# Cross-attention on one core: three GpSimd helpers of two instructions each become six of one, called in another order

## The reference, cut to what matters

```python
Q = (q @ Wq + bq).reshape(b, s, H, DH).transpose(0, 2, 1, 3)   # q = x
K = (k @ Wk + bk) ...; V = (v @ Wv + bv) ...                   # k = v = ctx
scores = jnp.einsum('bhqd,bhkd->bhqk', Q, K) / jnp.sqrt(jnp.float32(DH)) * mask
attn = jax.nn.softmax(scores, axis=-1)
ctx = jnp.einsum('bhqk,bhkd->bhqd', attn, V).transpose(0, 2, 1, 3).reshape(b, s, H * DH)
x = q + (ctx @ Wo + bo)
out = (x - mean(x)) * rsqrt(var(x) + LN_EPS) * gamma + beta
```

## Time and profile before

| | |
|---|---|
| median of 3 runs | 2428.19 us (2426.65 to 2430.57) |
| the profiled execution | 2422.3 us |
| its span, first to last instruction | 2420.5 us |
| TensorE busy | 2191.4 us, 91% |
| VectorE busy | 2016.7 us, 83% |
| ScalarE busy | 1792.0 us, 74% |
| GpSimd busy | 1100.5 us, 45% |

### The profile page before, as it was taken

How to read it: one execution, slowest core, us unless ns; L and a number is a source line. 1 busy time by engine, 2 the same in 40 slices (tenths; PEclk the granted TensorE clock), 3 DMA queues, 4 the chain that set the end, 5 groups by cost and what they waited for, 6 DMA issues and landing times.

```text
span 2420.5 us, 46357 instructions
## 1 busy us (share of the span) xinstructions
PE 2191.4 (91%) x12348; PEld 902.9 (37%) x12348; DVE 2016.7 (83%) x4283; ACT 1792.0 (74%) x3809; POOL 1100.5 (45%) x1576
## 2 busy tenths in 40 slices
PE   3789999999999999999999999999999999999995
PEld 1233433334333333433334333333433334333442
DVE  6798988889888888888889888888888889889892
ACT  3688786877868677786877868677786877868781
POOL 2134363544626355363544636355363544536434
PEclk9899999999999999999999999999999999999997
DMA  5388877687777868677687777868677687777774
GB/s 204 74 147 153 167 139 175 117 183 145 155 148 140 183 123 184 137 139 174 123 180 144 155 151 142 176 123 181 140 140 174 124 180 147 149 151 138 161 133 106
DMA packets 1117594, 363.28 MB, mean 150 GB/s; under 512 B 1073504, under 2 KB 1073504, under 8 KB 1117408
## 3 DMA queue, kind: packets, MB, share of 16 engines
q1 hardware_dynamic: 1114288, 361.58, 72.3%
q10 hardware_dynamic: 3120, 0.01, 0.1%
HBM read 76.30 MB, written 16.78 MB: 38 GB/s over the span
## 4 chain that ended last, share of the span: by engine, by line
PE 43%; ACT 17%; issue 17%; POOL 13%; DVE 7%; DMA 2%; ACTq 1%; POOLq 1%; DVEq 0%; SPq 0%
PE fill_ps L389 10%; PE fill_ps L390 9%; PE fill_ps L391 9%; PE score_ps L442 8%; ACT probs L614 7%; PE ctx_ps L463 6%; ACT p L628 5%; DVE p L939 3%; POOL neg_max L1234 2%; POOL raw L1214 2%; POOL acc L1276 2%; DVE score_ps L925 2%; ACT v L593 1%; DMA pT<-p 1%; POOL acc L1278 1%
## 5 line engine op out<-in xcount | busy, mean ns | idle before, releaser
L614 ACT ACTIVATE probs<-score_ps,neg_max 128x512 f32<-128x512 f32 x1024 | 694.5, 685 | 340.0 <-POOL neg_max L1234 295.5
L925 DVE CUSTOM_DVE_ANT_0 score_ps<-score_ps,mask_sb,small 128x512 f32<-128x512 f32 x1024 | 730.1, 752 | 72.3 <-PE score_ps L442 41.9
L939 DVE SCALAR_TENSOR_TENSOR p<-probs,inv_sum,p 128x512 f16<-128x512 f32 x896 | 758.3, 879 | 26.4 <-ACT p L628 26.4
L628 ACT ACTIVATE p<-probs,inv_sum 128x512 f16<-128x512 f32 x1024 | 681.3, 723 | 36.0 <-DVE inv_sum L933 33.6
L442 PE MATMUL score_ps<-k,q 64*128 64x512 f16 x3072 | 455.9, 387 | 142.7 <-ACT probs L614 135.8
L1234 POOL TENSOR_SCALAR neg_max<-row_max 128x2 f32<-128x2 f32 x512 | 179.0, 350 | 662.3 <-DVE row_max L925 659.4
L463 PE MATMUL ctx_ps<-pT,v 128*64 128x512 f16 x3072 | 360.8, 385 | 13.9 <-DMA pT<-p 12.4
L442 PEld LDWEIGHTS score_ps<-k,q 64*128 64x128 f16 x3072 | 142.5, 94 | 435.0 <-ACT probs L614 278.7
L1240 POOL TENSOR_SCALAR down_sum<-row_sum 128x4 f32<-128x4 f32 x256 | 74.5, 291 | 423.7 <-ACT probs L614 415.8
L463 PEld LDWEIGHTS ctx_ps<-pT,v 128*64 128x64 f16 x3072 | 166.3, 111 | 201.3 <-issue 72.5
L614 ACT ACTIVATION_READ_ACCUMULATOR probs<-score_ps,neg_max 128x1 f32 x1024 | 205.1, 200 | 0.0
(11 more groups left out here) (91 smaller groups left out, 3006.0 us busy)
## 6 DMA issues: line engine op xcount, KB each, us to landing
raw<-in_xt SPq DMA_DIRECT2D x64, 256.0 KB, 4.1
raw<-in_ct SPq DMA_DIRECT2D x64, 256.0 KB, 3.4
mask_sb<-in_mask_Bx1xSxS_fk SPq DMA_DIRECT2D x64, 256.0 KB, 3.1
acc<-in_x SPq DMA_DIRECT2D x64, 256.0 KB, 3.2
out<-acc SPq DMA_DIRECT2D x64, 256.0 KB, 2.5
pT<-p SPq DMA_TRANSPOSE x512, 4.5
wq_staged<-in_L_xattn_Wq SPq DMA_DIRECT2D x4, 512.0 KB, 6.9
wk_staged<-in_L_xattn_Wk SPq DMA_DIRECT2D x4, 512.0 KB, 10.8
```

The costliest lines, as they stand in the source:

```text
L614: nc.scalar.activation(probs[:, i % E_TILES, :], score_ps[:, i % 4, :], ACT.Exp, bias=neg_max[:, p % 2, i:i + 1], accum_out=row_sum[:, p % ...
L628: nc.scalar.activation(p16[:, q, a, 0, :], probs[:, i % E_TILES, :], ACT.Copy, scale=inv_sum[:, p % 2, i:i + 1]).then_inc(p_rounded, 1)
L925: nc.vector.tensor_tensor_reduce(out=score_ps[:, i % 4, :], in0=score_ps[:, i % 4, :], in1=mask_sb[:, q, :], scale=score_scale, scalar=-3. ...
L939: nc.vector.scalar_tensor_tensor(out=p16[:, q, a, 1, :], in0=probs[:, i % E_TILES, :], scalar=inv_sum[:, p % 2, i:i + 1], in1=p16[:, q, a, ...
```

## The change

`split_input` (L1214, L1217), `split_probs` (L1247, L1252) and `scale_and_shift` (L1276, L1278) are each cut in two. The new helpers are `scale_input` and `split_input`, `normalize_probs` and `split_probs`, `scale_out` and `shift_out`. No instruction is added or taken away, and each keeps its own waits. What differs is the place: GpSimd's `body` now calls the halves apart, and some negations of row maxima and scalings of sums stand between them. The other engines' programs are the same.

```diff
-            def split_input(n, t, tiles):
+            def scale_input(n, t, tiles):
...
+            def split_input(n, t, tiles):
+                for i in tiles:
                     wait_alone(pool, xc_scaled[t], n * DT + i + 1)
...
                 if here is not None:
+                    normalize_probs(here, 1, range(7, 8))
+                    negate_max(here, 2, range(2, 4))
                     split_probs(here, 1, range(7, 8))
-                    negate_max(here, 2, range(2, 4))
...
+                    normalize_probs(here, 3, range(7, 8))
+                    scale_sums(here, 4, 0)
                     split_probs(here, 3, range(7, 8))
-                    scale_sums(here, 4, 0)
...
-                    scale_and_shift(prev, range(0, 1))
+                    scale_out(prev, range(0, 1))
...
                     negate_max(here, 7, range(3, 4))
+                if prev is not None:
+                    shift_out(prev, range(0, 1))
+                if here is not None:
                     scale_sums(here, 7, 1)
                 if prev is not None:
-                    scale_and_shift(prev, range(1, 3))
+                    scale_out(prev, range(1, 3))
                 if nxt is not None:
                     negate_max(nxt, 0, range(0, 2))
...
                     scale_sums(nxt, 0, 1)
+                if prev is not None:
+                    shift_out(prev, range(1, 3))
+                if nxt is not None:
                     negate_max(nxt, 1, range(0, 1))
                 if prev is not None:
-                    scale_and_shift(prev, range(3, 4))
+                    scale_out(prev, range(3, 4))
                 if nxt is not None:
                     negate_max(nxt, 1, range(1, 2))
                     scale_sums(nxt, 1, 0)
+                    normalize_probs(nxt, 0, range(7, 8))
+                if prev is not None:
+                    shift_out(prev, range(3, 4))
+                if nxt is not None:
+                    negate_max(nxt, 1, range(2, 3))
                     split_probs(nxt, 0, range(7, 8))
-                    negate_max(nxt, 1, range(2, 4))
+                    negate_max(nxt, 1, range(3, 4))
```

More of the change, by code:

```diff
@@ L1249, in split_probs @@
                         p_normalized, 1)
+            def split_probs(n, p, tiles):
+                for i in tiles:
+                    q, a = i // 2, i % 2
                     sem_done, count = split_done(n, p, i)
@@ L1276, in scale_and_shift, with shift_out @@
                     nc.gpsimd.tensor_tensor(acc[:, q, :], acc[:, q, :], gamma_b[:, :], ALU.mult).then_inc(scaled, 1)
+            def shift_out(n, tiles):
+                for q in tiles:
+                    i = out_no(n, q)
                     pool.wait_ge(scaled, i)
@@ L1294, in body @@
                     negate_max(here, 3, range(2, 3))
+                    normalize_probs(here, 2, range(7, 8))
                     split_probs(here, 2, range(7, 8))
@@ L1316, in body @@
                 if nxt is not None:
-                    split_input(nxt, "x", range(0, 1))
+                    scale_input(nxt, "x", range(0, 1))
                 if here is not None:
@@ L1320, in body @@
                 if nxt is not None:
-                    split_input(nxt, "x", range(1, 2))
+                    split_input(nxt, "x", range(0, 1))
+                    scale_input(nxt, "x", range(1, 2))
                     scale_biases(nxt)
@@ L1325, in body @@
                 if nxt is not None:
-                    split_input(nxt, "x", range(2, 3))
+                    split_input(nxt, "x", range(1, 2))
+                    scale_input(nxt, "x", range(2, 3))
                 if here is not None:
@@ L1339, in body @@
                 if nxt is not None:
+                    split_input(nxt, "c", range(0, 1))
+                    scale_input(nxt, "c", range(1, 2))
+                if here is not None:
+                    negate_max(here, 7, range(0, 1))
+                if nxt is not None:
                     split_input(nxt, "c", range(1, 2))
                 if here is not None:
[L1342 removed]
+                    negate_max(here, 7, range(1, 2))
                 if nxt is not None:
[L1344 removed]
+                    scale_input(nxt, "c", range(2, 3))
+                    split_input(nxt, "c", range(2, 3))
+                    scale_input(nxt, "c", range(3, 4))
+                    split_input(nxt, "c", range(3, 4))
                 if here is not None:
@@ L1347, in body @@
                     negate_max(here, 7, range(2, 3))
+                    normalize_probs(here, 6, range(7, 8))
                     split_probs(here, 6, range(7, 8))
                     negate_max(here, 7, range(3, 4))
+                if prev is not None:
+                    shift_out(prev, range(0, 1))
+                if here is not None:
                     scale_sums(here, 7, 1)
                 if prev is not None:
-                    scale_and_shift(prev, range(1, 3))
+                    scale_out(prev, range(1, 3))
                 if nxt is not None:
@@ L1356, in body @@
                 if here is not None:
+                    normalize_probs(here, 7, range(7, 8))
                     split_probs(here, 7, range(7, 8))
```

14 lines of the change are left out of this document (9 added, 5 removed).

## The result

| | before | after |
|---|---|---|
| median | 2427.69 us (4 runs, 2426.65 to 2430.57) | 2282.46 us (4 runs, 2279.55 to 2285.32) |
| profiled execution | 2422.3 us | 2282.08 us |
| time as a share of before | 1 | 0.940 (0.9384 to 0.9416) |

The change makes the kernel 145 us, 6.0%, faster. One turn of the loop went from 145.2 to 135.3 us.

A forecast was written before the change was run, and what follows sets the result against it. TensorE, 91% busy, was taken as the bound, so only shorter pauses help. 15 x 4.46 + 14 x 1.5 = 88 us off the profiled 2422.3, plus 5.9 for the median, gave 2340 us; range 2302 to 2400.

The forecast's parts named there:

- place A: Pair 4's first sums, scaled ahead of tile 7's subtraction, come 1.2 us earlier; VectorE's idle goes, gain 0.86 us.
- place C: Next batch's pair 0: without two additions ahead, its first negation comes 2.6 us or more earlier; 1.5 us taken.
- rival 1: From the inputs' stretch on, ScalarE and VectorE become the bound: about half the gain, 2378 us; chance 0.26.
- Rival 3: VectorE's rests of probabilities collide more with GpSimd, 0.65 us each: slower, 2455 us; chance 0.07.
- rival 4: GpSimd is only a hop in the negation waits, so earlier handoffs wait elsewhere: no gain, 2428 us; chance 0.05.
- rival 2: Nearly the ceiling over the batch's pauses: 7.9 of 8.4 us a batch, 2310 us; chance 0.12.
- e: TensorE's pauses in pair 7's last two blocks: 0.9 of 2.0 us a batch expected to go.
- f: TensorE's pause at pair 0 of the next batch: 1.5 of 2.4 us a turn expected to go.
- a: TensorE's pause at pair 5: all of its 0.86 us a batch expected to go.
- b: TensorE's pause in pair 6's third block: all of its 1.1 us a batch expected to go.
- d: TensorE's pause in pair 7's first two blocks: 1.1 of 1.4 us a batch expected to go.
- c: TensorE's pause in pair 6's fourth block: 0.5 of 0.6 us a batch expected to go.

The follow-up runs named there:

- The outputs' part alone: Kernel before with only the gamma and beta steps (scaling and shifting of output blocks) in the new order: 2383.6 us, ratio 0.983.

## Why the prediction was right in kind and short in size

**Right.** All the named waits ended as said: at place A VectorE inverts at once, and in place C the first exponential follows without an idle time (3.17 us in the earlier trace rows). GpSimd and ScalarE at place C after:

```profile
1425.50 0.19 POOL L1237 TENSOR_SCALAR neg_max<-row_max 128x2 f32<-128x2 f32 x1 [0.28 <-DVE row_max L925]
```

```profile
1425.98 0.67 ACT L614 ACTIVATE probs<-score_ps,neg_max 128x512 f32<-128x512 f32 x1
```

SyncE's later store cost nothing that can be seen; and the later input planes stop no fill that they didn't stop before (`Q0` waits 6.2 us in all for them, 5.2 in before, nearly all of it once). ScalarE's waits for negations came to 176.3 (said: near 200), TensorE's for exponentials to 35.5 (said: near 70). Nothing of the result speaks for rival 1, 3 or 4. What came is rival 2 (below 2315 us, given 0.12): e and f went in full. But its 2310 us is still 28 us too slow, since it stopped at a ceiling of 8.4 us that was too low itself.

**The step that failed most: f (1.5 forecast, 2.9 measured).** A discount was wrong here. It said that VectorE "becomes what is late next" at f. Its four rests did follow there (in 2.73 us, 3.84 in before), but they delay no exponential that block f itself needs, and in the program two fills, some 5 us of matmuls, stand ahead of the next score block and cover them. I had read which engine is late next and not how long TensorE has other work. The outputs' part alone gave the whole 2.9.

**e (0.9 forecast, 2.03 measured).** The step "x4 in 5.37 us beside GpSimd's input work, which the change doesn't shorten" was wrong: 3.09 us after. Rival 3 took the same collisions with the wrong sign. The order within a collision changed: VectorE came first and GpSimd had to stand. The Trainium skill, "SBUF — State Buffer", section "Who interferes with whom", says that the order of issue decides who blocks. By that, the trace agrees: the four rests take 5.37 us where GpSimd's long scaling is 0.08 us ahead and 3.09 where VectorE is ahead of it, presumably since VectorE's four instructions follow each other without a gap, so that GpSimd finds no place between them. I had quoted that section for the count of collisions and not for their order. All of VectorE's rests of probabilities, on the page of after, take 60 us less than the 758.3 us of before, each 815 ns instead of 879:

```profile
L939 DVE SCALAR_TENSOR_TENSOR p<-probs,inv_sum,p 128x512 f16<-128x512 f32 x896 | 698.1, 815 | 1.0 <-ACT p L628 1.0
```

So "VectorE's busy time unchanged within some 20 us" missed by 40, on the good side.

**Mis-sized terms: a, b and d.** 1.11, 1.6 and 1.38 for 0.86, 1.1 and 1.1. For a the idle time in the bracket was taken without the 0.29 us that the modelled end hides; around b four stops ended that gave 0.13 to 0.67 us each on average, where the one batch shown gave me two; for d the cap by VectorE's mask didn't apply. **c: 0.5 forecast, 0 measured.** The 0.28 us stop is still there. It doesn't hang on these moves, and what sets it wasn't settled.

**Left out: g.** Pair 1's last blocks lose 0.55 us by the later addition. The prediction read that place only for harm.

**The loop's start.** That the change "doesn't touch it" was wrong: the place gave 2.0 us, 1.2 of them TensorE's stop, with ScalarE's pause going from 4.16 to 2.98 us on average, and 0.8 the clock that no longer falls in most turns. The prediction had no term for the clock. ScalarE's row after:

```profile
1323.92 0.69 ACT L602 ACTIVATE k<-fill_ps,bk_scaled 128x512 f16<-128x512 f32 x1 [2.95 <-issue]
```

But the stops behind it, where TensorE needs VectorE, whose own pause at the jump is as long as before (5.3 to 5.6 us), grew by 1.8. The net is some 0.2 us per turn, so this error alone moves the time by no more than 3 us.

**The sum.** a to g measure 9.6 us where the terms gave 5.96 and the stated ceiling 8.4. A ceiling of brackets in one batch plus 0.29 us for each was too low, by 0.25 in a, 0.5 in b, 0.5 in f and the whole of g, and 0.6 too high in c. With 15 batches of a to e (6.1 us), 14 of f and g (3.5 us) and the loop's start, this gives some 143 us of the 145. Had e and f been sized by the mechanism (2.0 and 2.4, their full brackets), the sum would be 8.0 us a batch and the time some 2311 us, inside the range; the other 29 us are the ceiling's error.

## What to carry to other kernels

- When an in-order queue serves a slow engine's short handoffs (here 0.2 us negations) between long instructions (1.2 us), put the handoffs between the long ones, so that no more than one of them stands ahead of a handoff; check the new wait by how much other work the bounding engine has ahead of its next need.
- Where VectorE and GpSimd slow each other down, read not only how many instructions collide but which comes first; here a tiny step (0.2 us) moved ahead went with the order being turned, and was worth 27 us.
- Look at which DMAs are issued just ahead of a hardware loop's jump. Holding them until the first instruction behind it took 19 to 30 us more off the changed kernel by the medians, and 14 to 26 by the ratios to before.
- A pause of TensorE can cost more than its length: look at the granted clock behind it, and compare starts of matmuls, not only idle time.

## What the hardware showed that I had not expected

- Four rests of 128 x 512 take 2.73 to 3.09 us when VectorE is ahead of GpSimd's scaling, and 5.37 us when that scaling is 0.08 us ahead; a GpSimd scaling takes 0.70 us alone and 1.77 behind them; even a 128 x 2 negation goes from 0.19 to 0.66.
- A jump to the loop's head stops ScalarE 2.0 us with SyncE quiet and 4.2 on average with loads and transposes in flight; VectorE 5.3 in before and 2.8 with only the transpose held.
- Behind TensorE's stop of some 3 us at the loop's start the granted clock fell to 0.50 in all 13 turns of before, and the matmuls there cost 0.8 us more; with the stop 1.2 us shorter it fell in 3 of 13.
- A hold on SyncE that delays 256 KB loads made the kernel faster although VectorE then waits up to 5.4 us for one of them.
